# A graph layer's gather loop: GpSimd's permitted lead over VectorE's add is changed from ten groups to four

## The reference

```
msg  = relu(x[src] + edge_attr @ We + be)                  # per edge, 128 features
aggr = segment_sum(msg, dst, 6250)
h    = relu(((1 + eps) * x + aggr) @ W1 + b1) @ W2 + b2
h    = (h - mean(h, 0)) * rsqrt(var(h, 0) + 1e-5) * gamma + beta
out  = layernorm(x + relu(h) + x)                          # per node
```

## Time and profile before

| | |
|---|---|
| median of 3 runs | 1920.73 us |
| the runs | 1918.39 to 1921.08 us |
| profiled execution, span from first to last instruction | 1919.8 us |
| mean granted TensorE clock | 0.861 of full speed |
| busy: PE, DVE, ACT, POOL | 1594.8, 1092.1, 317.4, 1427.4 us |

### The profile page before, as it was taken

How to read it: one execution, slowest core, us unless ns; L and a number is a source line. 1 busy time by engine, 2 the same in 40 slices (tenths; PEclk the granted TensorE clock), 3 DMA queues, 4 the chain that set the end, 5 groups by cost and what they waited for, 6 DMA issues and landing times.

```text
span 1919.8 us, 32224 instructions
## 1 busy us (share of the span) xinstructions
PE 1594.8 (83%) x10045; PEld 1234.0 (64%) x10045; DVE 1092.1 (57%) x1873; ACT 317.4 (17%) x555; POOL 1427.4 (74%) x1503
## 2 busy tenths in 40 slices
PE   1998888888988888888888898888888888888885
PEld 1876666666766666666666676666666666666664
DVE  3765555555555555555555555555555555555536
ACT  3311111111111111111111111111111111111135
POOL 7777777777777777777777777777777777777773
PEclk9988888888888888888888888888888888888887
DMA  8243333333333333333333333333333333333322
GB/s 228 71 96 85 83 84 83 82 83 83 82 84 82 82 84 82 83 83 82 84 82 82 84 82 83 83 82 84 82 82 84 82 83 83 82 84 83 82 70 75
DMA packets 85729, 165.36 MB, mean 86 GB/s; under 512 B 38885, under 2 KB 55098, under 8 KB 80586
## 3 DMA queue, kind: packets, MB, share of 16 engines
q0 software_dynamic: 47648, 97.65, 19.3%
q1 hardware_dynamic: 35164, 60.87, 14.6%
q10 hardware_dynamic: 2894, 6.57, 1.2%
HBM read 161.77 MB, written 3.20 MB: 86 GB/s over the span
## 4 chain that ended last, share of the span: by engine, by line
POOL 68%; issue 23%; DVE 2%; ACTq 2%; DMA 2%; ACT 1%; POOLq 1%; PE 1%; DVEq 0%
POOL xg L381 68%; DMA xg<-in_x,idxb 2%; ACTq L447 1%; POOLq L228 1%; DVE lnst L797 1%; DVE msg L632 0%; POOLq L229 0%; ACT x L476 0%; ACT accT L451 0%; PE ps L857 0%; ACT xT L453 0%; PE ps L879 0%; POOLq L268 0%; ACT msg L486 0%; PE ps L919 0%
## 5 line engine op out<-in xcount | busy, mean ns | idle before, releaser
L381 POOL DMA_INDIRECT xg<-in_x,idxb x1486 | 1413.0, 951 | 459.7 <-issue 450.1
L879 PE MATMUL ps<-x,sel 128*128 128x384 bf16 x3626 | 766.8, 370 | 64.9 <-DVE msg L641 64.2
L857 PE MATMUL ps<-hot,msg 128*128 128x64 f32 x3126 | 447.2, 291 | 215.9 <-ACT msg L486 206.1
L632 DVE TENSOR_TENSOR msg<-ps,xg 128x512 f32<-128x512 f32 (+1 forms) x390 | 259.0, 664 | 637.4 <-DMA xg<-in_x,idxb 614.6
L879 PEld LDWEIGHTS ps<-x,sel 128*128 128x128 bf16 x3626 | 387.6, 109 | 360.4 <-issue 168.8
L857 PEld LDWEIGHTS ps<-hot,msg 128*128 128x128 f32 x3126 | 441.2, 211 | 264.9 <-ACT msg L486 239.8
L656 DVE TENSOR_TENSOR sel<-srcb,ps 128x1664 bf16<-128x1664 int32 (+1 forms) x296 | 526.7, 1780 | 0.0
L486 ACT ACTIVATE msg<-msg 128x512 f32<-128x512 f32 x390 | 245.5, 630 | 1543.4 <-DVE msg L632 1271.4
L851 PE MATMUL ps<-wea,ea 65*128 65x128 f32 x3126 | 487.5, 305 | 1.3 <-issue 1.3
L851 PEld LDWEIGHTS ps<-wea,ea 65*128 65x128 f32 x3126 | 430.5, 213 | 6.6 <-issue 6.4
L622 DVE TENSOR_TENSOR hot<-rel,ps 128x256 f32<-128x256 f32 x390 | 163.5, 419 | 27.0 <-issue 15.6
(11 more groups left out here) (85 smaller groups left out, 153.3 us busy)
## 6 DMA issues: line engine op xcount, KB each, us to landing
ea<-in_eat SPq DMA_DIRECT2D x78, 640.0 KB
xg<-in_x,idxb POOLq DMA_INDIRECT x1486, 2.5
srcb<-in_src_row SPq DMA_DIRECT2D x74, 64.0 KB
xT<-in_xt ACTq DMA_DIRECT2D x1, 3125.0 KB, 19.0
out<-iota_all SPq DMA_DIRECT2D x5, 512.0 KB
idxb<-in_src_loop SPq DMA_DIRECT2D x78, 10.0 KB
hot_all<-in_dst_tiles SPq DMA_DIRECT2D x1, 781.0 KB, 4.4
out<-iota_all SPq DMA_DIRECT2D x2, 256.0 KB
```

The costliest lines, as they stand in the source:

```text
L381: pool.indirect_dma_start(out=xg[0:rows, slot, j, :], out_offset=None, in_=x, in_offset=bass.IndirectOffsetOnAxis(ap=index, axis=0)).then_ ...
L632: last = dve.tensor_tensor(msg[:, g % 2, 0:G, :], ps_lin(g % 2)[:, 0:G, :], xg[:, g, 0:G, :], ALU.add)
L857: last = pe.matmul(ps_win(k), msg[0:r, k, j, :], hot[0:r, k, j, :], start=(j == 0), stop=(j == len(tiles) - 1))
L879: last = pe.matmul(ps[:, 7, 0:3 * HID], sel[:, q % 2, b, :], x3[:, b0 + b, :, :].rearrange("p a h -> p (a h)"), start=(b0 + b == 0), stop= ...
```

## The change

GpSimd's wait ahead of a group asks for the add of the group four before it, in place of ten before it, and it now also stands ahead of groups 4 to 9, which had none. Nothing else is edited: the ten slots of `xg` and all other waits stay.

```diff
     AHEAD = 1
+    BEHIND = 4
     CH = 484
...
-                    if not isinstance(i, int) or i:
-
-                        wait_apart(pool, s_pre, (i - 1) * SLOTS + g + 1)
+                    if not isinstance(i, int) or i * SLOTS + g >= BEHIND:
+
+                        wait_apart(pool, s_pre, i * SLOTS + g + 1 - BEHIND)
                     for j in range(GROUP - special(i, g)):
                         gather(g, j, P, idxb[h][:, at + j:at + j + 1], s_xg[g])
```

## The result

The changed kernel took 1936.70 us in the median of four runs (1935.37 to 1938.74), the kernel before, measured beside it, 1919.56 us: ratio 1.0095, 95% interval 1.008 to 1.0109. It is 17.1 us slower. The forecast was 1937.2, which is 16.5 over the 1920.7 that it started from; its range was 1933.5 to 1942.

What follows compares the result with a forecast made beforehand. GpSimd, making DMAs without a pause, was taken to bound the kernel. 21.3 - 5.2 - 1.3 - 4.9 + 7.1 - 0.5 = 16.5 us on the median of 1920.7 gave 1937.2 us, range 1933.5 to 1942.

Steps and rivals of the forecast that it cites:

- The pause before group 5: Start: group 5's first gather waits for the add of group 1, moving from 29.66 to about 51.0: +21.3 us.
- the load of x: Start: without group 5's gathers beside it, its 26 us issue shortens: -0.5 us, bounds 0 and -1.
- The wait of group 10: Start: the old idle time before group 10, for its index list, does not come again: -5.2 us.
- Old holds: Start: gathers formerly held by VectorE's L664, one at 48.41 and others from 61 to 81 us, given back: -1.3 and -4.9 us.
- New holds: Start, from 51 us on: seven L664 each hold one gather of the now unbroken GpSimd: +7.1 us, bounds 2.7 and 11.5.
- The layout against the old starts: Start: the new holds laid out against the L664 starts, 7.5 us; the mean was taken instead.
- The loop's wait: Mid-loop: the stricter wait is met before it is read, margin 10.2 us at the tightest group seen: cost 0.
- The first (cheaper gathers): Making of each DMA: gathers get cheaper with fewer in flight, so the kernel is not slower; 1916 at 15 ns each; 3%.
- The second (another cause of the holds): Start: the holds have another cause than L664 and do not come again: 9.4 us, so 1930.1; 4%.
- The third (a load of x quicker by 5 us): Start: the pause lets ScalarE's chain end 5 us sooner: 1932; 3%.
- The fourth (a bite in the loop): Loop: the new wait bites once for each of 74 special tiles; at 1 us each, 2011; 3%.
- The fifth (no such lead): GpSimd never had such a lead when it matters, so the change does nothing: 1920.7; 1%.

Runs made afterwards that it cites:

- start_only: The kernel before with only the six new waits of groups 4 to 9, the loop's wait as before: 2983.6 us against 2963.2, ratio 1.0062.
- after_again: The changed kernel, unchanged, run and profiled again: 2581.7 us against 2960.7 for the kernel before, ratio 0.871.
- behind3: The changed kernel with three groups of lead in place of four: 2584.6 us against 2956.3 for the kernel before, ratio 0.8742.
- behind2: The changed kernel with two groups of lead in place of four: 2567.8 us against 2956.3 for the kernel before, ratio 0.8703.
- one_in_four: The kernel before with one gather for each group, the other tiles' rows set to zero: 1541.5 us against 1917.7, ratio 0.8049.
- idx_early: The kernel before with SyncE's load of the index list moved ahead of its wait for TensorE: 2569.2 us against 2956.3, ratio 0.8709.
- best: The kernel before with idx_early's edit and loop_only's wait together: 1915.84 us against 1917.68, ratio 0.9988.
- before_again: The kernel before, unchanged, profiled once more: 2965.1 us, ratio to its like 1.0006.
- no_hold: The changed kernel with L665's second operand from PSUM in place of SBUF (wrong remainders): 2581.4 us against 2963.2 for the kernel before.
- loop_only: The kernel before with the four-behind wait only from iteration 2 on, the start as before: 2583.3 us against 2963.2, ratio 0.8688.

## Why the prediction was right, point by point

The time, its sign and its place were right, and so was the mechanism: a pause at the start of an engine that bounds the rest. All the terms can be read in the trace of after. That 1936.7 came within 0.5 us of 1937.2 is luck in part: the start cost 18.3 us in the trace and not 16.5, and the forecast started from 1920.7, 1.2 over the median measured beside the change.

- **The pause before group 5**: forecast +21.3, and -0.5 for the load of x, together 20.8. Measured 50.22 - 29.66 = 20.6, by luck, as two errors cancel. The restart takes 0.80 us, not the 0.2 for which the prediction gave no row (0.81 at the eight pauses of start_only, after_again, behind3 and behind2): +0.6. And the add of group 1 ended 1.35 us earlier, 49.42 in place of 50.77. Of this 0.86 is that L448 was issued at 8.15 us in place of 9.01, before any new wait, so it isn't the change; 0.50 is that the issue took 25.50 in place of 26.00. Is that 0.5 the pause's? Kernels without a pause have 26.00, 26.17, 27.70, 25.16, 25.64 and 26.00 us, mean 26.1; those with the pause at groups 4 and 5 have 25.50, 24.37, 25.38, 25.66 and 26.76, mean 25.5; behind3 and behind2, which pause earlier, 24.70 and 23.78. one_in_four, with a quarter of the gathers beside the load, has 24.98. Fewer gathers beside the load go with a shorter issue, but the two means differ by less than the runs within each, so the size of 0.5 is not shown.
- **The wait of group 10**, -5.2: gone, as forecast. That it was the index list and not the add was shown by idx_early and best: both leave group 10's wait for the add as it was, move that load ahead, and lose the pause.
- **Old holds**, -1.3 and -4.9: read from rows of before, both gone.
- **New holds**: forecast +7.1 with bounds 2.7 and 11.5; measured over 0.94 us: 1.40 + 1.62 + 1.26 + 1.62 + 0.54 + 1.59 + 1.12 = +9.1. This is the term that was off most. Seven L665 caught one gather each, as forecast, and each such gather ended 0.81 or 0.82 us after its L665 (53.59 + 1.89 = 55.48, and 53.96 + 2.34 = 56.30). What failed is the mean over the offset: it took the offsets as even, and they are not. VectorE's L665 come in pairs 2.87 us apart (53.59 and 56.46), and the gather behind the first one's hold starts at 56.60, 0.14 us into the second, which makes a nearly full hold, 2.56; the pair of 61.45 and 64.32 does the same. after_again, in its start, has the same seven within 0.07 us. The layout against the old starts, 7.5, was somewhat nearer and was passed over.
- **Sum of the start**: 20.6 - 5.2 - 1.3 - 4.9 + 9.1 = 18.3 us; forecast 16.5. In the profile 3.5 us of this are covered by the quicker cadence (the distance from gather to gather) and 0.9 by a shorter end (41.7 us from the last gather's start to the end of the span, before 42.6), which leaves 13.9 for the 13.8 of the spans. The medians, over four runs each, differ by 17.1.
- **The loop's wait**, 0: right in A. In mid-loop the margin was forecast at 10.2 us; after, it is 10.5 at such a place (an add over at 1018.82, and a first gather at 1029.32 that asks for it). But one place was taken for the tightest, and it wasn't: over all groups from 20 to 379 the trace of before has 6.6 us at the least (group 20, its first gather at 113.66, the add of group 16 over at 107.05), and the changed kernel 9.7. The margin was there all the same. The two rows of the 10.5:

```profile
1018.13 0.69 DVE L633 TENSOR_TENSOR msg<-ps,xg 128x512 f32<-128x512 f32 x1 [3.16 <-DMA xg<-in_x,idxb]
```

```profile
1029.32 0.94 POOL L382 DMA_INDIRECT xg<-in_x,idxb  x1 [0.30 <-issue]
```

- **The signs.** The pauses, the seven holds and the missing gap before group 10 came. Off were the end of the long pause, 50.22 in place of 50.5 to 51.0; its length, 18.1 in place of 19, and that of the short one, 3.0 in place of 2; and the last gather, 14.65 us later in place of 16.5. A gather's mean in the loop is 0.943 us in place of 0.945, which the prediction had named as a sign of being wrong; it goes with the execution and not with the wait, as the 1.2482 of before_again shows.
- **The rivals.** The first (cheaper gathers) fell with before_again. The second (another cause of the holds) fell with no_hold and L657: three rows of before had shown the 0.83 us, and no_hold took the cause away. The Trainium skill (SBUF — State Buffer, "Who interferes with whom") infers that tensor_tensor doesn't stall descriptor generation; here it did, seven times by up to 1.6 us, so the measurement decides. The third (a load of x quicker by 5 us) was 0.5 us. The fourth (a bite in the loop) did not happen in A. The fifth (no such lead) fell with the pause itself, 18.12 us.

What the prediction did not see is that its starting point, that GpSimd bounds the kernel and nothing gives the loss back, belongs to condition A. In B TensorE bounds it, and the same change is worth -12.9%. Two edits that have in common that GpSimd no longer waits for its index list once in a part (the four-behind wait, and idx_early) give the same 13%, and start_only, which leaves that wait, gives none of it. That much is shown. Why the long wait goes with another 500 us of TensorE's issue, and what starves the issue at all, is open: the two kernels that were to tell it ran in A.

## What to carry to other kernels

A limit on an engine's lead costs nothing where the engine has no lead, and all of it where the lead is the stock for a known pause of its consumer; so cost it at the start, and check the margin in the middle at many groups, the first ones above all (the one place taken here for the tightest was not the tightest). When the limited engine is the bound and never idle later, each us of pause at the start is a us at the end, minus the stalls that the old start had there, plus those that the new one meets. Read what a wait is really for before counting it: here the profile named the add, and it was an index list held back by a wait that it did not need. Taking that wait away gave 13% in B by itself, and in A, together with a loop wait that costs nothing, 1.8 us.

## What the runs showed of the hardware

- Making a gather's DMA that starts while a VectorE tensor_tensor of 1.5 to 1.9 us with both operands in SBUF runs is held until 0.81 to 0.83 us after that operation's end (7 of 7 in the changed kernel; in loop_only one that started within 0.01 us of the operation was not). With one operand in PSUM it isn't held, the length of the operation being the same: none of ten in no_hold, and none beside the 296 L657 of the changed kernel.
- GpSimd takes 0.80 us from the end of the add that it waits for to the start of its next gather; where the semaphore is already there, the gap is 0.30 us.
- The distance from gather to gather differs between executions, 1.248 to 1.251 us, which is some 4 us over 1430 gathers; two profiles of this kernel can't be compared below that.
- In one_in_four TensorE is busy 91% of the span and its mean granted clock is 0.975 of the upper level, 2.4 GHz; in the kernel before it is busy 83%, at 0.861. A selection matmul (L879, here L874) takes 336 ns in place of 370.
- The same program on the same chip took 2960.7 and 1917.7 us within ten minutes, with 949 us of TensorE's idle time put down to its own issue in place of 1.5, and a granted clock of 0.721 in place of 0.861 (the traces before_again and before). A kernel's rank can turn round between the two: the change is 0.95% slower in one and 12.9% faster in the other.
